# Where the products with the values stand among the maxima: two runs per tile in the grouped layers

## The reference

```python
xn = x * rsqrt(mean(x * x) + 1e-5) * norm_w
q = (xn @ wq)                       # 16 heads of 32
k, v = ctx @ wk, ctx @ wv           # 4 heads of 32
scores = einsum(q, k) / sqrt(32)
attn = softmax(scores)
x = x + (attn @ v) @ wo
```

## Time and profile before

| | us |
|---|---|
| median of 3 runs | 4637.84 (4637.76 to 4638.88) |
| the profiled execution, its own time | 4637.64 |
| its span, first to last instruction | 4635.9 |
| PE busy | 4336.0 (94%) |
| DVE busy | 2565.3 (55%) |
| ACT busy | 1986.6 (43%) |
| POOL busy | 1809.3 (39%) |

### The profile page before, as it was taken

One profiled execution on the slowest core, in us unless ns is written; L12 is line 12 of the kernel. 1 busy time (PEld: TensorE's weight loads), 2 busy tenths in 40 slices (PEclk: granted clock), 3 DMA queues, 4 the chain that ended last, 5 costly groups with the idle time before them and its releaser, 6 DMA issues. The chain is left out here.

```text
span 4635.9 us, 63591 instructions
## 1 busy us (share of the span) xinstructions
PE 4336.0 (94%) x20066; PEld 2694.6 (58%) x20066; DVE 2565.3 (55%) x3575; ACT 1986.6 (43%) x2444; POOL 1809.3 (39%) x923
## 2 busy tenths in 40 slices
PE   7999799996999999999978999999999998999998
PEld 6888588883556555655644554544554554455454
DVE  2122200014555455545447777787777777777776
ACT  2111211112333333333325566566656656666665
POOL 0000000002353444344434556555555555555655
PEclk9999899997999999999988999999999999999999
DMA  4333422224444444444442223322322322232233
GB/s 155 130 127 131 155 80 82 79 88 131 107 115 115 109 102 120 115 109 113 107 125 62 81 73 90 88 83 81 92 81 75 94 84 86 82 88 79 77 95 97
DMA packets 301729, 461.95 MB, mean 100 GB/s; under 512 B 44955, under 2 KB 95131, under 8 KB 301693
## 3 DMA queue, kind: packets, MB, share of 16 engines
q1 hardware_dynamic: 301692, 461.50, 34.4%
HBM read 227.88 MB, written 102.76 MB: 71 GB/s over the span
## 5 line engine op out<-in xcount | busy, mean ns | idle before, releaser
L813 DVE TENSOR_REDUCE a_max_cols<-a_ps 128x1 f32<-128x512 f32 x2072 | 1323.4, 677 | 329.4 <-PE a_ps L937 327.0
L707 ACT ACTIVATE a_probs<-a_ps 128x1024 f32<-128x1024 f32 x1024 | 1018.6, 1027 | 735.8 <-PE a_ps L958 732.7
L937 PE MATMUL a_ps<-a_k_ops,a_q_ops 96*128 96x512 f32 (+1 forms) x2592 | 955.0, 433 | 42.7 <-DVE a_max_cols L813 30.9
L937 PEld LDWEIGHTS a_ps<-a_k_ops,a_q_ops 96*128 96x128 f32 (+1 forms) x2592 | 459.8, 190 | 627.0 <-DVE a_max_cols L813 490.9
L958 PE MATMUL a_ps<-a_q_ops,a_k_ops 128*128 128x512 f32 x2560 | 780.0, 407 | 36.3 <-ACT a_probs L707 20.7
L595 POOL TENSOR_TENSOR a_probs<-a_probs 128x1024 f32<-128x1024 f32 x192 | 463.3, 2413 | 726.9 <-PE a_ps L974 705.7
L974 PE MATMUL a_ps<-a_probs,a_v 128*32 128x512 f32 (+1 forms) x4096 | 674.6, 610 | 0.0
L958 PEld LDWEIGHTS a_ps<-a_q_ops,a_k_ops 128*128 128x128 f32 x2560 | 462.5, 190 | 215.7 <-ACT a_probs L707 104.4
L595 POOL TENSOR_TENSOR a_sums<-a_probs 128x1024 f32<-128x1024 f32 x192 | 454.3, 2385 | 5.0 <-ACT a_probs L707 5.0
L595 POOL TENSOR_TENSOR a_sums<-a_sums,a_probs 128x1024 f32<-128x1024 f32 x192 | 455.2, 2390 | 0.3
L601 POOL TENSOR_TENSOR a_qn_lo<-a_qf,a_qn_hi 128x512 fp32r<-128x512 f32 x99 | 126.7, 1280 | 791.2 <-ACT a_qn_hi L662 791.2
(11 more groups left out here) (92 smaller groups left out, 5615.5 us busy)
## 6 DMA issues: line engine op xcount, KB each, us to landing
a_k_ops<-k_scratch SPq DMA_DIRECT2D x201, 256.0 KB, 4.0
a_q_ops<-a_qn_hi SPq DMA_DIRECT2D x792, 64.0 KB, 2.0
k_scratch<-kp_out SPq DMA_DIRECT2D x88, 512.0 KB, 2.8
a_q_ops<-a_qn_hi SPq DMA_DIRECT2D x268, 128.0 KB, 2.3
a_x_raw<-out_t SPq DMA_DIRECT2D x26, 1024.0 KB, 5.3
a_q_ops<-a_qn_lo SPq DMA_DIRECT2D x396, 64.0 KB, 2.0
a_x_res<-out_t SPq DMA_DIRECT2D x96, 256.0 KB, 3.1
out_t<-a_results SPq DMA_DIRECT2D x96, 256.0 KB, 2.0
```

Of the source, the lines that this page charges most:

```text
L707: act.activation(probs[:, s], ps[:, 2 * (s % 2):2 * (s % 2) + 2, :], ACT.Exp)\
L813: dve.tensor_reduce(max_cols[:, col:col + 1], bank(MAXB[n]), AX.X, ALU.max, negate=True).then_inc(reduced, 1)
L937: last = pe.matmul(bank(MAXB[n]), q_ops[0:rows(p), s, h, p, q * P:(q + 1) * P], k_ops[0:rows(p), s, k_head(h), p, :], start=(p == 0), stop ...
```

## The change

In the grouped layers `outputs` of quarters 0 and 1 stand one behind the other at the end of step 3, and quarters 2 and 3 behind the last of the maxima, directly ahead of the denominators. Layer 0 keeps its places. The wait for the mean square's reading of bank 6 (`ms_step`) moves with quarter 0 into `outputs`.

```diff
-    OUT_AT = (2, 3, 5, NS - 1) if has_norm else (1, 2, 3)
+
+    OUT_AT = {3: (0, 1)} if has_norm else {1: (0,), 2: (1,), 3: (2,)}
+    OUT_LAST = [kt for kt in range(KT) if not any(kt in kts for kts in OUT_AT.values())]
...
                     pe.wait_ge(normed, 1 + it * T + t)
+                    if has_norm and t == 0:
+                        pe.wait_ge(ms_step, MS * (it + 1) + 1)
                 pe.wait_ge(exped, (it * T + t) * NS + (kt + 1) * (H // 2))
...
                     for r in range(NS):
-                        if has_norm and r == NS - 1:
-                            outputs(it, t, KT - 1)
...
-                        if r in OUT_AT and not (r == NS - 1 and has_norm):
-                            if has_norm and t == 0 and r == OUT_AT[0]:
-                                pe.wait_ge(ms_step, MS * (it + 1) + 1)
-                            outputs(it, t, OUT_AT.index(r))
-                    if not has_norm:
-                        outputs(it, t, KT - 1)
-                    else:
+                        for kt in OUT_AT.get(r, ()):
+                            outputs(it, t, kt)
+                    for kt in OUT_LAST:
+                        outputs(it, t, kt)
+                    if has_norm:
                         denominators(it, t)
```

## The result

| | before | after |
|---|---|---|
| median of 4 runs, us | 4638.11 (4637.76 to 4638.88) | 4723.99 (4720.03 to 4726.46) |
| profiled execution, own time | 4637.64 | 4726.46 |
| its span | 4635.9 | 4724.7 |

The ratio is 1.0184 (95% interval 1.0166 to 1.0202): the change makes the kernel 86 us slower. The forecast was 42 us slower, 4680, with 4655 to 4705 as its range; the time lies above it.

A forecast was written before the change was run, and what follows sets the result against it. PE, busy 94%, was taken to bound the kernel, with DVE slower inside the maxima. Per pass 1.92 - 0.92 + 0.21 + 0.21 = +1.42 us, over 24 passes +34, plus 8 for the clock: 4637.8 + 34 + 8 = 4680 us, range 4655 to 4705.

The forecast's parts named there:

- Tile 3, +0.21: Tile 3: 1.05 us saved on changes of form is lost to PE's waits in maxima 12 to 15; +0.21 us.
- Tile 0, +1.92: Tile 0: DVE, with four more pieces, loses 0.48 us; DVE then PE work alone, so the turn comes 1.92 us later.
- the walk: The prediction's step-by-step account of a tile, following PE and DVE through waits for banks; +1.42 us a pass.
- rival D: Runs don't join: each quarter stays at 1.00 us even next to another; +40 us, 4712; chance 0.03.
- Tile 1 into tile 2, -0.92: End of tile 1: the split comes 1.37 us earlier, exponential 0 of tile 2 0.92 us earlier; -0.92 us for both.
- a sign of being wrong: PE's wait for the split (L819) was to be nearly gone; one as long as before would show the forecast wrong.
- The clock, +8: Tile 0: the granted clock falls behind PE's waits in the last four maxima, in one of five passes; +8 us.
- its own bound for more falls: The forecast's mechanism, at 0.80, included falls of the clock between none and two in three passes.
- The passes that load weights, counted like the rest (+4): The three passes that also load weights were counted like the others, at +1.42 us each.
- A: Rival: PE stays the bound, bank waits are shorter, at most 0.5 us saved per tile; 4590 us; chance 0.05.
- B: Rival: inversions fall into DVE's wait for maxima 8, so tile 0 costs only 0.21 us; 4631 us; chance 0.06.
- C: Rival: the clock falls in nearly all passes, 41 us on top; 4713 us; chance 0.06.

The follow-up runs named there:

- experiments 3 and 4: The changed kernel with only quarters 0 and 1 joined (3), 4634.3 us; with only quarters 2 and 3 joined behind maxima 15 (4), 4727.6 us.
- experiment 7: The changed order in tiles 1 to 3 only, tile 0 as in the kernel before; 4651.5 us, ratio 1.0032.
- experiments 8 and 9: In the grouped layers each reduction reads 256 of 512 columns: in the kernel before (8), 4620.3 us; in the changed kernel (9), 4631.9 us.
- experiment 1: The changed kernel, with POOL in tile 1 waiting for split_x before taking the rest of the output; 4702.5 us, ratio 1.0143.
- experiment 2: The changed kernel, with tile 0's matmuls of maxima 12 and 14 done twice and of 13 three times; 4694.6 us, ratio 1.0126.
- experiment 5: The kernel before, with POOL in tile 1 waiting for split_x before taking the rest of the output; 4625.7 us, ratio 0.9970.
- Experiment 10: The changed kernel with POOL waiting for split_x in tile 1 and maxima 12 to 14 of tile 0 repeated; 4678.3 us, ratio 1.0089.

## Why the prediction was wrong in size and right in direction

- **Tile 3, +0.21:** right. Measured +0.19, and experiments 3 and 4 give its two halves, -0.35 for the early join and +0.53 for the late one.
- **Tile 0, +1.92:** right. Where the clock doesn't fall, measured 32.83 against 30.93, +1.90, with the waits where the walk has them; experiment 7 shows that this tile carries most of the change, and with half reductions (experiments 8 and 9) it is +0.11.
- **Runs that join (against rival D):** right, 1.86 and 3.57 us.
- **Tile 1 into tile 2, -0.92: this step failed.** The prediction moved the split's start by 1.37 us and kept its 2.67 us. The duration was not the split's own: 0.52 us of it was a wait for POOL's last instruction, and by starting earlier it met all of that instruction and 0.57 us of the sum ahead of it. Counted from maxima 5 of tile 1, which starts at 3302.45 before and 3428.34 after, the split's end stands at 12.60 us and PE's first matmul behind it at 12.77 in both. The wait for the split stayed at 1.2 us where it was 1.4, and the prediction had named such a wait as a sign of being wrong. 20 passes x 0.87 us make 17 us; experiment 1 gives back 19. The row was there to be read: 2.27 us is the shortest split of the grouped layers before, 2.65 the median, and POOL's L605 lies beside the long ones. The Trainium skill (SBUF — State Buffer, "Who interferes with whom") has the rule: a DVE instruction with two SBUF inputs contends with a GpSimd instruction that reads SBUF, and what they share is an exclusive lock. The traces agree, with 2.15 us from the end of the POOL instruction that held the split to the split's end in all 42 passes without weights of the two kernels. I had looked at POOL only for its sums.
- **The clock, +8: right mechanism, size off by three.** The term took one fall in five passes; there were 15 in 21 at some 1.65 us, 25 us in all; experiment 2 gives back 27 by filling the waits. The prediction had the 1.9 us of waits in maxima 12 to 15 right, and its own bound for more falls was two in three; but for the forecast it leaned on the row nearest to no fall, a single wait of 1.41 us behind a full stretch. The later runs lie nearer to its other row (2.02 us of waiting, a fall): 1.9 us in pieces brought a fall in 15 of 21 tiles, a single wait of 1.8 in 12 of the 19 passes that have it (experiment 9).
- **The passes that load weights, counted like the rest (+4):** they cost 12 us. Their stretches at a clock of 0.50 add up to 75 us in the profile after and 55 before, and at half the rate the 20 us more would be about 10 us. No run takes these passes apart, so that is argued and not shown. Nor is it shown why experiment 5 brings their tile 1 from 25.1 us in the mean to 22.9.
- **Before the grouped layers:** 3.7 us of the profiled executions' difference lie there, where both have the same order. The first turn of the grouped layers was between 2440 and 2449 us in the ten experiments; so this reads as spread and not as the change.

The missed terms are 17 (the split) + 17 (the clock, 25 - 8) + 8 (the passes with weights, 12 - 4) + 4 (ahead of the grouped layers) = 46 us on top of the 42 forecast: 88, where the profiled executions differ by 89. All miss in the same direction, so none hides another. Experiment 10 takes out the split's term and the falls in tile 0 and lands at 4678, 41 us above the kernel before.

Of the rivals, A fell at once, and B with tile 0's +1.90. In favour of A, experiments 8 and 9 show that tiles 1 and 3 do gain 0.4 to 0.5 us where DVE is fast enough. C named the right place with too high a count, a fall in nearly every pass; its 4713 lies nearer to the measured time than the forecast because its surplus of falls (41 - 25 = 16 us) stands in for the split's missing 17, which would have been luck.

## What to carry to other kernels

Joining small matmuls of one form saves a real 0.35 us per change of form here, but work that stands between the uses of a few rotating banks is also the cover under which the engine that empties them catches up. Walk both engines from bank to bank before joining, tile by tile: the same join brought 0.35 us in tile 3 and cost 0.73 in tile 0. And before a step is moved earlier, compare its shortest and its usual duration: if they differ, part of the row may be a wait that shows nowhere else. Then an earlier start makes the row longer and the end no earlier; the rows that lie beside the long ones on the other engines say whose work it waits for.

## What the runs showed of the hardware that was not expected

- DVE's 128x2048 subtraction of two SBUF tensors takes 2.28 us alone, and as far as the rows show it makes no progress while POOL runs a `tensor_tensor`: 2.67, 4.00 and 5.40 us, each ending 2.15 behind POOL. Where one POOL instruction follows the other at once, either can come next: in the profile after, the split was held past the change from the sums to L607 in 20 of the 21 passes that met it, in experiment 9 in 19 of 21; in the others it got in between, and POOL's 1.27 us became 3.33 to 3.35. Ahead of the grouped layers, in the kernel before, a split got in between two POOL instructions 0.08 us apart (L583), and the second took 3.19. What decides it is not shown.
- Four matmuls more in each tile 0, with nothing else changed, made the kernel 27 us faster: the granted clock stayed at 1.00 over the 3.6 us of matmuls behind the wait in all 21 tiles, where it had fallen in 15.
